# Weighing v in pairs of steps, a first split on GpSimd, and maxima sent straight to their rows, in a two-kind transformer kernel

## The reference

```python
x = x + 0.5 * ffn(layernorm(x));  x = x + attn(layernorm(x));  x = x + 0.5 * ffn(layernorm(x))

def attn(x):        # 16 heads of 4, on the left 64 columns
    q, k, v = (left @ W.T for W in (Wq, Wk, Wv));  att = softmax(q k^T / scale);  return (att v) @ Wo.T + bo
def ffn(src):       # 16 heads of 8, then a mixture of experts
    q, k = rope(src @ Wq), rope(src @ Wk_c @ Wk);  v = src @ Wv_c @ Wv
    x = rmsnorm(src + (softmax(q k^T / sqrt(8)) v) @ Wo, norm1_w)
    shared = swiglu(x @ W_shared_in) @ W_shared_out
    h = swiglu(x @ W1_shared);  routed = sum_e (h @ W2_experts[e]) * w[:, e]   # top 2 of a group of 4
    return rmsnorm(x + shared + routed, norm2_w)
```

## Time and profile before

| what | value |
|---|---|
| median of three runs | 864.01 us |
| profiled execution, its own time | 863.97 us |
| its span, first to last instruction | 862.2 us |
| mean granted TensorE clock | 0.976 |
| busy: PE, DVE, ACT, POOL | 810.3, 672.4, 498.6, 349.9 us |
| first exp of units 0, 1, 2, 3, 4 | 47.0, 109.7, 189.1, 266.3, 341.3 us |
| first exp of units 5, 6, 7, 8 | 414.1, 461.1, 508.5, 560.3 us |
| first exp of units 9, 10, 11; last exp | 613.5, 689.7, 762.3; 828.4 us |

### The profile page before, as it was taken

How to read it: one execution, slowest core, us unless ns; L and a number is a source line. 1 busy time by engine, 2 the same in 40 slices (tenths; PEclk the granted TensorE clock), 3 DMA queues, 4 the chain that set the end, 5 groups by cost and what they waited for, 6 DMA issues and landing times.

```text
span 862.2 us, 13324 instructions
## 1 busy us (share of the span) xinstructions
PE 810.3 (94%) x4362; PEld 305.2 (35%) x4362; DVE 672.4 (78%) x1311; ACT 498.6 (58%) x1063; POOL 349.9 (41%) x766
## 2 busy tenths in 40 slices
PE   3589999999999999999998999999999999999995
PEld 2122334434333333333322223233344344345453
DVE  5786998778759767876989998899986688683356
ACT  1045775456537636753787777767764475377441
POOL 2163425462543354254333434325143813443453
PEclk9587999999999999999999999999999999999999
DMA  3453311120100010001011130403102200000000
GB/s 109 139 148 90 88 61 47 31 73 3 47 32 1 22 58 3 2 21 59 3 40 40 45 109 22 128 8 94 60 15 62 76 15 2 2 14 3 1 13 13
DMA packets 25048, 38.81 MB, mean 45 GB/s; under 512 B 6596, under 2 KB 22212, under 8 KB 23372
## 3 DMA queue, kind: packets, MB, share of 16 engines
q1 hardware_dynamic: 23873, 36.25, 14.6%
q10 hardware_dynamic: 1107, 1.72, 0.6%
HBM read 28.01 MB, written 9.50 MB: 44 GB/s over the span
## 4 chain that ended last, share of the span: by engine, by line
PE 71%; DVE 14%; POOL 5%; ACT 4%; issue 4%; DMA 3%; ACTq 0%; POOLq 0%; DVEq 0%
PE ps_out L818 16%; PE ps L757 13%; PE ps L791 12%; PE ps L882 11%; DVE maxes L972 9%; PE ps L867 6%; PE ps L737 2%; ACT probs L1153 2%; PE ps_out L807 2%; PE ps L779 2%; PE ps L874 2%; PE ps L744 1%; PE ps L845 1%; DVE src L1052 1%; DMA max_parts_rows<-maxT 1%
## 5 line engine op out<-in xcount | busy, mean ns | idle before, releaser
L1153 ACT ACTIVATE probs<-ps 128x512 f32<-128x512 f32 x768 | 416.8, 596 | 256.1 <-PE ps L791 233.0
L972 DVE TENSOR_REDUCE maxes<-ps 128x1 f32<-128x512 f32 x768 | 481.1, 681 | 67.8 <-PE ps L757 66.1
L757 PE MATMUL ps<-k_aug,q_aug 72*128 72x512 bf16 (+1 forms) x768 | 259.0, 392 | 17.7 <-DMA k_aug<-qk_parts 14.8
L791 PE MATMUL ps<-q_aug,k_aug 75*128 75x512 bf16 (+1 forms) x704 | 243.6, 385 | 6.1 <-DMA q_aug<-max_parts_rows 3.1
L818 PE MATMUL ps_out<-probs,v_aug 128*18 128x512 f32 x1408 | 187.1, 604 | 4.4 <-ACT probs L1153 3.1
L757 PEld LDWEIGHTS ps<-k_aug,q_aug 72*128 72x128 bf16 (+1 forms) x768 | 66.0, 98 | 190.9 <-issue 140.7
L882 PE MATMUL ps<-w,hidden 128*128 128x512 f32 x256 | 118.4, 596 | 1.0 <-DVE hidden L1029 1.0
L791 PEld LDWEIGHTS ps<-q_aug,k_aug 75*128 75x128 bf16 (+1 forms) x704 | 61.5, 97 | 136.3 <-issue 78.9
L1065 DVE TENSOR_TENSOR prod<-ps,gate 128x512 f32<-128x512 f32 x56 | 38.7, 691 | 58.8 <-PE ps L882 51.3
L1257 POOL TENSOR_SCALAR max_parts<-maxes 128x16 bf16<-128x16 f32 (+1 forms) x38 | 10.3, 271 | 151.1 <-DVE maxes L972 151.1
L1347 POOL TENSOR_TENSOR prod<-prod 128x512 f32<-128x512 f32 x28 | 35.5, 1268 | 73.3 <-DVE prod L1065 43.5
(11 more groups left out here) (127 smaller groups left out, 739.3 us busy)
## 6 DMA issues: line engine op xcount, KB each, us to landing
q_aug<-qk_parts SPq DMA_DIRECT2D x7, 1152.0 KB
k_aug<-qk_parts SPq DMA_DIRECT2D x21, 384.0 KB
qk_parts<-parts SPq DMA_DIRECT2D x45, 128.0 KB, 2.3
q_aug<-qk_parts SPq DMA_DIRECT2D x12, 288.0 KB
k_aug<-qk_parts SPq DMA_DIRECT2D x24, 96.0 KB
qk_parts<-parts SPq DMA_DIRECT2D x24, 64.0 KB, 2.0
k_aug<-qk_parts ACTq DMA_DIRECT2D x12, 96.0 KB
X<-in_x_dram SPq DMA_DIRECT2D x4, 256.0 KB, 4.2
```

The lines of the kernel that those rows point to most:

```text
L757: pe.matmul(bank(use[i]), q_aug[p0:p1, r, at, qt * 128:(qt + 1) * 128], k_aug[p0:p1, r, at, :], start=True, stop=True).then_inc(bank_full[ ...
L791: pe.matmul(bank(use[i]), k_aug[p0:p1, r, at, kt * 128:(kt + 1) * 128], q_aug[p0:p1, r, at, :], start=True, stop=True).then_inc(bank_full[ ...
L972: dve.tensor_reduce(maxes[:, u % 2, qt, at:at + 1], full(use[0]), AX.X, ALU.max).then_inc(bank_free[use[0][0]], 1)
L1153: act.activation(probs[:, step % P_RING, c:c + exp_run(u), :], both(use), ACT.Exp, scale=scale)\
```

## The change

Six things change.

1. Weighing v runs two steps at a time in units 0, 1, 2, 3, 9 and 10, and there are three buffers of probs in place of two in all units. The space comes from qf, attn and attnT: the rotated q or k now lies in rope_s, the attention output and its transpose in prod (in rope_c and rope_s for the last unit). The first heads_out of a unit therefore waits for the expert sums of the unit before, which use prod.
2. In unit 0, DVE rotates q and k one after the other and splits only k; POOL splits q. k has its own buffers (in hidden) and its own semaphore. The later q_aug loads of unit 0 wait for the first piece of k_aug to have landed, and not for the stores of k.
3. The maxima of wide units go from maxT to q_aug in one DMA (new L740). Their parts are laid out by part, head and tile for that. Attention units still go through DRAM.
4. In the turns of units 4 and 7 (TOGETHER_UNITS), the exp tiles and the maxima tiles are put at even places, so that they come in pairs.
5. Every unit has PREP and POST tables of its own, MAX_LATE moves by up to four places, and HOLD, which the bank model uses, is new.
6. PE always turns max_parts at its full 128 columns.

```diff
-VECTOR_SPLITS = {0}
+VECTOR_SPLITS = {(0, 1)}
+TOGETHER_UNITS = {4, 7}
-P_RING = 2
+P_RING = 3
+DOUBLE_UNITS = {0,1,2,3,9,10}
-PREP_SECOND = {"norm_stats": [22], "norm_apply": [26], "x_transpose": [51], "qk_project": [54, 64],
-               "qk_split": [62, 73], "v_project": [65], "stack": [65, 78]}
+PREP_1 = {"norm_stats": [19], "norm_apply": [32], "x_transpose": [49], "qk_project": [54, 65], "qk_split": [62, 75],
+          "v_project": [61], "stack": [71, 75]}
...
-MAX_LATE = [39, 33, 23, 14, 16, 18, 22, 24, 25, 21, 15, 18, 14]
+MAX_LATE = [41, 33, 24, 18, 16, 17, 22, 24, 25, 21, 18, 15, 12]
...
+def together(place):
+    return place - place % 2 if place // TILES in TOGETHER_UNITS else place
...
-        for s in range(TILES // 4):
+        for s in range(steps_at_once(u) - 1, TILES // 4, steps_at_once(u)):
             late = u * TILES + 4 * s + 3 + WEIGH_LATE
             put(late, "weigh_v", u, s)
...
+        def rotate(eng, seq, own_wait, u, qk):
+            c, s, q = rotated(u, qk)
+            seq(eng.tensor_tensor(s, s, sinT[:, :], ALU.mult))
+            own_wait()
+            if u:
+                eng.wait_ge(part_done, parts_before(u, qk))
+            return eng.tensor_tensor(q, c, s, ALU.add)
...
-                    if u + i == 1 and i:
-                        k_stored(queue)
+                    if u == 0 and i == 1:
+                        queue.wait_ge(first_loaded[0], 16 * FIRST_DMAS)
...
+                    if is_ffn(u):
+                        p0 = product_rows(u)
+                        sp.dma_start(q_aug[p0:p0 + PARTS, r, at, :].rearrange("c h (t q) -> c (h t) q", q=128),
+                                     maxT[0:TT * PARTS * n, :].unsqueeze(1)).then_inc(max_loaded[i], 16)
+                        continue
...
-                    s, = args
-                    g, kt, n = s // TT, s % TT, u * 16 + s
-                    taken(pe, "exp_scores", u, s, 4 - exp_run(u))
+                    last, = args
+                    taken(pe, "exp_scores", u, last, 4 - exp_run(u))
+                    for s in range(last - steps_at_once(u) + 1, last + 1):
+                        n = u * 16 + s
...
+                    if u == 0:
+                        released(dve, use[0])
+                        rotate(dve, seq, own_wait, u, qk).then_inc(first_rotated, 1)
...
+                        if is_ffn(u - 1) and u < LAST:
+                            experts_added(dve, u - 1)
```

More of the change, by code:

```diff
@@ L172, in max_rows_before, with narrow_rows_before @@
     return sum(max_pieces(v) for v in range(u))
+def narrow_rows_before(u):
+    return sum(max_pieces(v) for v in range(u) if not is_ffn(v))
 def slot_dmas(u, i):
@@ new lines @@
+POST_3 = {"heads_out": [3, 3], "heads_transpose": [6], "out_project": [8], "rms_stats": [11, 63], "rms_apply1": [17],
+          "x1_transpose": [18], "logits": [23], "mlp_up": [27, 30, 30, 34],
+          "router": [25, 28, 33, 40, 42, 43, 43, 44], "shared_out": [39], "expert": [44, 47, 48, 51, 51, 51, 55, 56],
+          "rms_apply2": [68], "ffn_out": [68]}
+POST_4 = {"heads_out": [4, 4], "heads_transpose": [7], "out_project": [15], "attn_out": [31]}
+POST_5 = {"heads_out": [4, 7], "heads_transpose": [15], "out_project": [20], "attn_out": [23]}
@@ new lines @@
+POST_6 = {"heads_out": [2, 3], "heads_transpose": [6], "out_project": [19], "attn_out": [29]}
+POST_7 = {"heads_out": [3, 3], "heads_transpose": [9], "out_project": [10], "attn_out": [52]}
+POST_8 = {"heads_out": [3, 3], "heads_transpose": [8], "out_project": [10], "rms_stats": [11, 71],
+          "rms_apply1": [15], "x1_transpose": [19], "logits": [24], "mlp_up": [22, 32, 34, 38],
+          "router": [28, 34, 35, 35, 37, 37, 38, 39], "shared_out": [35], "expert": [41, 42, 46, 49, 53, 60, 61, 63],
+          "rms_apply2": [77], "ffn_out": [86]}
@@ L301, in max_place @@
     start, end = ((v - 1) * TILES + MAX_LATE[v] for v in (u, u + 1))
-    if u and (is_ffn(u) != is_ffn(u - 1) or u in MAX_PAIRS):
+    if u and (is_ffn(u) != is_ffn(u - 1) or u - 1 in TOGETHER_UNITS or u in MAX_PAIRS):
         m += 1 - m % 2
-    return start + m * (end - start) // TILES
+    return together(start + m * (end - start) // TILES)
+def together(place):
+    return place - place % 2 if place // TILES in TOGETHER_UNITS else place
 def plan():
@@ L370, in macaron @@
         rope_s = sb("rope_s", [128, S])
-        qf = sb("qf", [128, S])
-        rest = rope_c
         parts = sb("parts", [128, 2, PARTS, S], BF16)
@@ L396, in macaron, with attention @@
         prod = sb("prod", [128, 2, 2, EPG, C])
+        def attention(u):
+            if u >= LAST:
+                return rope_c, rope_s
+            return (prod[:, 0, i, :, :].rearrange("p e c -> p (e c)") for i in range(2))
         logit = sb("logit", [128, TT, E_GRP + E])
@@ L837, in _ @@
                     o = bank(use[0])
+                    attn, _ = attention(u)
                     for t in tiles:
@@ L843, in _ @@
                     o = bank(use[0])
+                    _, attnT = attention(u)
                     for t in tiles:
@@ L1122, in _ @@
                     qk, = args
-                    act.wait_ge(part_done, PARTS * (2 * u + qk))
-                    ins = act.activation(qf[0:rows, :], full(use[0])[0:rows, :], ACT.Copy)
+                    act.wait_ge(part_done, parts_before(u, qk))
+                    ins = act.activation(rope_s[0:rows, :], full(use[0])[0:rows, :], ACT.Copy)
                     ins.then_inc(bank_free[use[0][0]], 1)
@@ L1243, in _ @@
                     pool.tensor_tensor(rstd[:, :], var_eps[:, :], power[:, :], ALU.pow).then_inc(rstd_done, 1)
-                elif name == "qk_split" and u not in VECTOR_SPLITS:
+                elif name == "qk_split" and (u, args[0]) not in VECTOR_SPLITS:
                     split(pool, seq, own_wait, u, *args)
```

215 lines of the change are left out of this document (117 added, 98 removed).

## The result

The kernel after takes 859.45 us (median of 4 runs, 858.44 to 860.05) beside 864.45 us for the kernel before on the same chip: ratio 0.9938, 95% interval 0.9913 to 0.9964. On another chip it was 859.84 us beside 863.76, ratio 0.9947 (0.9916 to 0.9978). The forecast was 845.9 us, range 837 to 858. The direction holds; of 18 us 5 came.

A forecast was written before the change was run, and what follows sets the result against it. PE was taken to set the time, with the start a case by itself. Terms -2.4 - 1.7 - 1.65 - 3.0 - 6.6 - 2.7 = -18.05 from 863.97 gave 845.9 us, range 837 to 858.

The forecast's parts named there:

- The start: Start and unit 0, up to the first exp of unit 1: 8.75 us shorter.
- split and hop: Before the first exp: POOL splitting q takes 2.4 us off the path, one DMA hop fewer for the maxima 1.7.
- up to 1.6 us more: Load of k's first piece at the start: less traffic could shorten it by this much; not in the -2.4 taken.
- Hops and clock: Direct maxima DMA: -1.7 at the first piece, -1.65 in PE's wait for the second, -3.0 from full clock behind it.
- By that row the fall goes away: Unit 0, second maxima piece: with the wait cut to 1.2 us the clock stays full; -3.0 taken of 4.85 us.
- Pairs of weighing, -6.6: Units 1, 2, 3, 9, 10: 40 pairs save PE 0.22 us each, 8.8 us; three quarters taken.
- I count two of a unit's eight pairs as lost to DVE: Wide units other than unit 0: DVE limits two of eight weighing pairs, cutting 8.8 us to 6.6.
- The fourth rival: Weighing pairs starve the readers of score tiles, DVE losing up to 0.6 us a pair: slower, 875 us; chance 0.06.
- its turning point: Loss per weighing pair that would cancel the whole forecast gain: 18 / 48 = 0.38 us.
- DVE bound: Whole kernel: DVE limits, so pairs, unit 7's second half and clock give nothing; -5.75, 858.2 us; chance 0.19.
- Pairs of tiles, -2.7: Units 4 and 7: attention tiles side by side save PE 25 turns of 0.22 us, 5.5 us; half taken.
- The rest at nothing: Freed tensors, new tables and the tail: heads_out's added wait and moved places, tail -1 to +1 us; taken as 0.

The follow-up runs named there:

- the old tables: Kernel after with PREP, POST, MAX_LATE and HOLD of before and no even places: 867.06 us with pairs of weighing, 856.11 us with single steps.
- the new tables alone: Kernel after with single weighing steps in all units (DOUBLE_UNITS empty), all else kept: 857.27 us, beside 859.93 us for the kernel after on the same chip.
- pairs alone: Kernel after with places, MAX_LATE and HOLD of before and no even places in units 4 and 7, pairs of weighing kept: 867.06 us.

## Why the prediction was wrong

- **The start** was right in sum, and that was luck: first exp of unit 1 at 99.9 us for 109.7, 9.8 us against 8.75. Up to the first exp 2.9 us came of the 4.1 for split and hop, and in unit 0 6.9 of 4.65. The split gave 1.6 us at the first maxima for 2.4: DVE and POOL slowed each other. The load of k, expected to bring "up to 1.6 us more", brought 2.3. In two other profiles of the kernel after the half clock at the start was longer and unit 1 began at 103.0 and 103.9 us, so the start is worth 5.8 to 9.8.
- **Hops and clock** (-1.7, -1.65, -3.0): near in the old tables. The hop taken back costs 2.2 us at the first exp, of which 0.7 is there at the first maxima already, and 1.73 in the wait; the rest of 4.7 us in unit 0 is clock. In the kernel after the hop brought nothing at the first exp: from the first maxima to PE's first exp tile it is 15.96 us for 15.60. The reason given for the clock does not hold: "By that row the fall goes away" rests on a wait of 1.68 us in the tail behind which the clock stayed at 1.00. At the same place in the kernel after, behind 1.69 us, it fell to 0.50 (below).
- **Pairs of weighing, -6.6: this step failed.** "A second step right behind the first should not pay it: 0.22 us a pair" holds (0.21). Measured are +2.0 us in the five units. What failed is "I count two of a unit's eight pairs as lost to DVE". I priced the readers by their idle time over a unit, where 16 to 19 us looked ample. The waits are local: a pair shuts both off for 1.85 us, then eight tiles each arrive in 3.5 us where DVE needs 5.0 and ACT 4. The fourth rival had this mechanism, priced it for DVE alone, and had a chance of 0.06. Its price, "up to 0.6 us a pair", holds: 0.34 in the old tables. But I set its turning point at 0.38, against all the gains; for the pairs as a term it is 0.22, and by that the term should have been given zero or a loss. Here lie 8.6 us of the miss. Pairs and new tables cannot be cleanly parted in it: by the account PE waits 10.0 us in these units before, 14.8 with the new tables alone, 24.0 with pairs alone and 19.7 with both, where its work is some 9 us less. So about half of the added waits of the kernel after stand with single steps too, and are the tables'.
- **The rival next to the result.** "DVE bound" had 858.2 us, 1.3 from the 859.45 measured, but its mechanism is not what happened: the clock term paid, PE's work did fall, and DVE is idle 16 us in unit 10 as before.
- **Pairs of tiles, -2.7**: units 4 and 7 by themselves gained 2.1 us in the run of this edit alone, near the forecast, but unit 5 gave 2.0 back. In the kernel after two falls of the clock cost unit 4 up to 2.7 more (73.5 us for 70.8 in its twin without pairs, where they are absent). Net -0.7.
- **The rest at nothing**: +3.4 us. In the tail, 35.2 us, some 3.3 is clock by the account, and it is 33.5 us in a profile with a fall half as long. Unit 11 is 1.7 us longer by its new tables.
- **"A clock of 1.00 from 50 us on"** was a check for the start alone. I had no term for falls elsewhere: before had none from 74 to 859 us, after has four.

Of the checks, DVE's wait for PE was the right one to name, but its bar was too high. With pairs in the old tables it doubled in unit 10, 5.3 to 11.0 us. In the five units of the kernel after it is 40.8 us for 31.3 before, 0.24 us a pair: under the 0.38 that was to show the forecast wrong, and over the 0.21 that a pair saves.

## What to carry to other kernels

Work saved on the bounding engine counts only where its readers can take the results at the new rate within the few buffers between them; compare rates and buffers over one round (here eight tiles and seven banks) and not idle time over a stage. Bunching work that gives the readers nothing must be priced as a gap for every reader and as a rush behind it, and its turning point is its own saving, not the gain of the whole change. Judge a bundle by taking its parts apart: here the small edits of the start earned all, and an order retuned for the headline edit hid what that edit cost.

## What the runs showed of the hardware

- The clock can fall long after the start, right behind a short wait: with pairs and old tables the granted clock was 0.50 for 3.4 us behind a wait of 1.00 us (685.57), and in the kernel after behind one of 0.68 us, with attention tiles and small float32 matmuls around it. On the timeline of PE of after:

```profile
349.94 0.85 PE L806 MATMUL ps<-awq,xT 64*128 64x64 f32 x6 [0.68 <-DVE maxes L1041]
...
351.18 1.91 PE L880 MATMUL ps_out<-probs,v_aug 128*18 128x512 f32 x8
```

  The wait does not decide it. Behind 1.47 us at 58.42 the clock stayed at 1.00, behind 1.43 us at the same place with the old tables and single steps it fell. In the tail it stayed behind 1.68 us in the kernel before and fell behind 1.69 us in the kernel after:

```profile
835.75 1.03 PE L923 MATMUL ps<-w_gate,x1T 128*128 128x10 f32 x4 [1.69 <-ACT x1T L1273]
```

  The fall at 334.0 us in the kernel after has no more than 0.19 us of waiting in the 3 us before it, and the one at 279.4 none. What decides stays open.
- Half clock differs between executions of one kernel. In the first 67 us it is 27.3, 37.5 and 41.0 us in three profiles of after; the falls in units 3 and 4 stand at the same places in the first two, and only one of the three is in the last. The mean granted clock of the kernel after goes from 0.964 to 0.975 on one chip, and its time from 865.35 to 857.32 us.
- The direct DMA of maxima takes 2.74 us on the chain of the run with the first split on DVE, where the store takes 2.35 and the second hop 1.69 in the run through DRAM. Between the first maxima and PE's first exp tile the two hops cost 1.4 us more than the direct way (16.80 and 15.38 us, old tables, single). In the second profile of the kernel after the direct DMA takes 3.14 us. The forecast took 1.92, and the 2.56 that it had beside it was nearer.
- DVE and POOL side by side on SBUF operands slow each other: on DVE 0.44 to 1.20 us for a cast and 0.70 to 1.26 for a multiply, on POOL 0.61 to 0.95 for a cast and 1.15 to 1.48 for a subtraction.
